# A graph network's edge pass: TensorE fetches the eighth tile of neighbour rows in two steps of three, by one-pass float32r products

## The reference, cut to what matters

```python
q = x @ Wq + bq ; k = x @ Wk + bk ; v = x @ Wv + bv ; e = eattr @ We
kj = k[src] + e                                   # rows of k fetched by source node
alpha = sum(q[dst] * kj, -1) / sqrt(C)
a = softmax of alpha over the edges of one destination
out = segment_sum(a * (v[src] + e), dst) + x @ Ws + bs
```

## Time and profile before

| | |
|---|---|
| runs, median of 3 | 6549.0 us (6548.15 to 6552.57) |
| the profiled execution's own time | 6551.77 us |
| its span | 6550.1 us |
| TensorE, matmul | 5681.8 us busy (87%) |
| VectorE | 4841.0 us (74%) |
| GpSimd | 4534.8 us (69%) |
| ScalarE | 2723.7 us (42%) |
| mean granted TensorE clock | 0.860 |

### The profile page before, as it was taken

How to read it: one execution, slowest core, us unless ns; L and a number is a source line. 1 busy time by engine, 2 the same in 40 slices (tenths; PEclk the granted TensorE clock), 3 DMA queues, 4 the chain that set the end, 5 groups by cost and what they waited for, 6 DMA issues and landing times. The chain is left out here.

```text
span 6550.1 us, 181005 instructions
## 1 busy us (share of the span) xinstructions
PE 5681.8 (87%) x44238; PEld 3448.3 (53%) x44238; DVE 4841.0 (74%) x17139; ACT 2723.7 (42%) x12085; POOL 4534.8 (69%) x4907
## 2 busy tenths in 40 slices
PE   7997888888888888888888888888888888888887
PEld 5775555555555555555555555555555555555554
DVE  6556777777777777777777777777777777777777
ACT  3223444444444444444444444444333333333332
POOL 1223777777777775777777777775777777777775
PEclk9998888888888888888888888888888888888887
DMA  4554333333333343333333333333333333333333
GB/s 128 159 159 107 98 98 98 98 98 98 98 98 100 96 100 101 98 98 99 98 98 99 99 97 99 97 99 101 100 98 98 98 98 98 98 98 98 98 98 81
DMA packets 710753, 668.87 MB, mean 102 GB/s; under 512 B 395660, under 2 KB 532814, under 8 KB 710702
## 3 DMA queue, kind: packets, MB, share of 16 engines
q0 software_dynamic: 154880, 306.75, 19.1%
q1 hardware_dynamic: 526730, 308.56, 17.7%
q10 hardware_dynamic: 29092, 52.97, 2.7%
HBM read 645.88 MB, written 21.78 MB: 102 GB/s over the span
## 5 line engine op out<-in xcount | busy, mean ns | idle before, releaser
L1830 POOL DMA_INDIRECT Gall<-KV,sdn x4638 | 4397.5, 948 | 1438.6 <-issue 1374.4
L1100 PE MATMUL pG<-KVS,oh 128*128 128x512 f32 (+1 forms) x5226 | 2971.0, 725 | 24.1 <-DVE lm L838 2.0
L1100 PEld LDWEIGHTS pG<-KVS,oh 128*128 128x128 f32 x5226 | 1200.6, 241 | 1404.9 <-issue 1390.7
L1141 ACT ACTIVATE vals<-vj,vals 128x32 f32<-128x32 f32 (+1 forms) x7960 | 1794.8, 312 | 19.3
L1134 ACT ACTIVATE vals<-dd 128x16 f32<-128x16 f32 (+1 forms) x606 | 131.7, 217 | 3247.0 <-DVE dd L963 3219.4
L884 DVE TENSOR_TENSOR kj<-Gall,pE 128x512 f32<-128x512 f32 x603 | 408.5, 678 | 477.3 <-DMA Gall<-KV,sdn 467.0
L1088 PE MATMUL pY<-O,vals 128*66 128x42 f32 (+1 forms) x10576 | 755.6, 233 | 0.0
L1088 PEld LDWEIGHTS pY<-O,vals 128*66 128x66 f32 (+1 forms) x10576 | 683.2, 139 | 47.0 <-ACT vals L1148 35.4
L1073 PE MATMUL pY<-fw,Ob 128*42 128x6 bf16 (+1 forms) x4800 | 211.1, 166 | 448.2 <-DVE cr L936 447.3
L873 DVE SCALAR_TENSOR_TENSOR oh<-kb,prow,pM 128x512 f32<-128x512 int16 (+1 forms) x606 | 472.4, 780 | 21.2 <-DMA kb<-K 19.0
L1021 PE MATMUL pE<-bd,ea 64*128 64x128 f32 x4848 | 465.8, 314 | 16.9 <-PEq L1414 16.2
(11 more groups left out here) (253 smaller groups left out, 6398.1 us busy)
## 6 DMA issues: line engine op xcount, KB each, us to landing
db<-D SPq DMA_DIRECT2D x606, 256.0 KB, 3.8
ea<-in_ea SPq DMA_DIRECT2D x606, 128.0 KB
Gall<-KV,sdn POOLq DMA_INDIRECT x4638
db<-D ACTq DMA_DIRECT2D x202, 256.0 KB, 3.6
qw<-QT SPq DMA_DIRECT2D x1818, 5.2 KB
dr<-in_dr SPq DMA_DIRECT2D x1212, 4.0 KB
ea<-in_ea SPq DMA_DIRECT2D x202, 64.0 KB, 3.5
sdn<-in_sdn SPq DMA_DIRECT2D x606, 12.0 KB
```

The source lines that it names most:

```text
L1100: p = e.matmul(pG[:, 0:128 * m], oh[s.slot][:, n, :], KVS[:, 4 * q:4 * q + m, :].rearrange("p t c -> p (t c)"), start=k == 0 and n == 0, s ...
L1141: i = e.activation(vals[u][:, j, C * h:C * h + C], vj[u][:, j, C * h:C * h + C], ACT.Identity, scale=vals[u][:, j, 64 + h:65 + h])
L1830: e.indirect_dma_start(G[u][:, j, :], None, kvtab, bass.IndirectOffsetOnAxis(ap=sdn[u][:, j:j + 1], axis=0)).then_inc(s_g[u], 16)
```

## The change

GpSimd leaves out the eighth gather in two blocks of three: blocks A (3, 6, ...) and B (4, 7, ...). Block A's pick ("early") is made a step ahead of the block, in stage Z between d and cont, and block B's where the pick was. There are two tables of keys (`kb[0]`, `kb[1]`) and two one-hot tables of 13 quads (`ohA`, `ohB`). In a step with block A in stage A, `p_gp` fetches quads 4 to 12 of B's fetch; with block B it waits for B's pick and fetches quads 0 to 8 of the next A fetch; with the third block a new operation `p_gq` behind q fetches A's quads 9 to 12, then, behind aT and A's pick, `p_gp` fetches quads 0 to 3 of B's. `v_oh` makes 9 quads in two of the steps and 4 + 4 in the third.

Each quad is now two products in float32r, one with the upper and one with the lower part of the table: `KVH` (in place of `KVS`) and `KVL` (over `hT`), made in the late loop by ScalarE (`upper_A`, `upper_in_place_A`) and VectorE (`lower_V`). As `hT` is overwritten, GpSimd sets its rows of ones again in the next table phase ("one"). VectorE's edge pass also waits for the end of ScalarE's table phase.

```diff
+    ohA = nc.alloc_sbuf_tensor_at("ohA", [128, QUADS, 128], F32R, offset=nc.sbuf_base - 256 * NT)
+    KVH = nc.alloc_sbuf_tensor_at("KVH", [128, NT, 128], F32R, offset=nc.sbuf_base - 512 * NT)
+    KVL = nc.alloc_sbuf_tensor_at("KVL", [128, NT, 128], F32R, offset=nc.sbuf_base - 512 * NT)
...
-    oh = [sb(f"oh{u}", [128, PIECE[2], 128]) for u in range(3)]
+    kb = [sb(f"kb{x}", [128, 128], I16) for x in "AB"]
+    ohB = sb("ohB", [128, QUADS, 128], F32R)
...
+        def upper_A(e, c):
+            if c >= 3:
+                e.wait_ge(own["A"], pA["kh", c - 3])
+            e.activation(part(c), KVS[:, cells(c), :], ACT.Copy).then_inc(own["A"], 1)
+
+        def upper_in_place_A(e, c):
+            e.wait_ge(own["V"], pV["kl", c])
...
+            e.activation(KVH[:, cells(c), :], part(c).bitcast(F32), ACT.Copy).then_inc(own["A"], 1)
...
+        def lower_V(e, c):
+            e.wait_ge(own["A"], pA["th", c])
+            e.wait_ge(own["P"], pP["qs", c])
+            e.tensor_tensor(KVL[:, cells(c), :], KVS[:, cells(c), :], part(c).bitcast(F32),
+                            ALU.subtract).then_inc(own["V"], 1)
...
-        first_pick = 2 + z.peel
-        pick_slot = first_pick % 3
+        pick_A, pick_B = 2 + z.peel, 3 + z.peel
+        slot_A, slot_B = pick_A % 3, pick_B % 3
...
         def picks(s):
 
-            return s.slot == pick_slot and not (isinstance(s.i, int) and s.c < first_pick)
+            return s.slot in (slot_A, slot_B) and not (isinstance(s.i, int) and s.c < first_of(s))
...
-            after(e, "P", "gp", s - 1)
+            if u == slot_A:
+                after(e, "P", "gq", s)
+            else:
+                after(e, "P", "gp", s - 1)
...
+        def hot(e, table, x, f, t):
+            return e.scalar_tensor_tensor(
+                table[:, f:t, :], kb[x][:, :].unsqueeze(1).to_broadcast([128, t - f, 128]), prow[:, 0:1],
+                pQd[:, f:t].unsqueeze(2).to_broadcast([128, t - f, 128]), ALU.subtract, ALU.is_equal)
+
         def v_oh(e, s):
...
+            if s.slot == slot_B:
+                key_landed(e, s + 2)
+                return hot(e, ohA, 0, 0, CUT_A)
+            if s.slot == slot_A:
+                return hot(e, ohB, 1, CUT_B, QUADS)
+            hot(e, ohA, 0, CUT_A, QUADS)
+            key_landed(e, s + 2)
+            return hot(e, ohB, 1, 0, CUT_B)
...
+        def fetch(e, table, f, t):
+            for n in range(f, t):
+                q = order_q[n]
+                m = min(4, NT - 4 * q)
+                for h, half in enumerate((KVH, KVL)):
+                    p = e.matmul(pG[:, 0:128 * m], table[:, n, :],
+                                 half[:, 4 * q:4 * q + m, :].rearrange("p t c -> p (t c)"),
+                                 start=n == 0 and h == 0, stop=n == QUADS - 1 and h == 1)
+            return p
+
         def p_gp(e, s):
...
+            if s.slot == slot_A:
+                return fetch(e, ohB, CUT_B, QUADS)
+            if s.slot == slot_B:
+                if picks(s):
+                    after(e, "V", "sel", s)
+                    hold(e)
+                return fetch(e, ohA, 0, CUT_A)
+            after(e, "V", "early", s + 1)
+            hold(e)
+            return fetch(e, ohB, 0, CUT_B)
+
+        def p_gq(e, s):
+            after(e, "V", "oh", s - 1)
+            hold(e)
+            return fetch(e, ohA, CUT_A, QUADS)
```

More of the change, by code:

```diff
@@ L7 @@
 F32 = mybir.dt.float32
+F32R = mybir.dt.float32r
 I32 = mybir.dt.int32
@@ L472, in node_phase @@
             if folds:
-                oG += [("clr", c) for c in fo]
+                oG += [(o, c) for c in fo for o in (("one", "clr") if kind == "mid" else ("clr",))]
                 for c in fo:
@@ L497, in node_phase @@
             oP += [(o, c) for o in q_P]
-            oA += [(o, c) for o in q_A]
-            oV += [(o, c) for o in q_V]
+            oA += [(o, c) for o in q_A + ["th"]] + ([("kh", c - 2)] if c >= 2 else [])
+            oV += [(o, c) for o in q_V + ["kl"]]
+        if late:
+            oA += [("kh", NG - 2), ("kh", NG - 1)]
         pV, pP, pA, pG_ = place(oV), place(oP), place(oA), place(oG)
@@ L556, in rows_P @@
             e.wait_ge(own["A"], pA["col", c])
+            if kind == "mid":
+                e.wait_ge(own["G"], pG_["one", c])
             if c >= 2:
@@ L593, in scalar @@
                 query_A(e, c)
+                upper_A(e, c)
+                if c >= 2:
+                    upper_in_place_A(e, c - 2)
+            if late:
+                upper_in_place_A(e, NG - 2)
+                upper_in_place_A(e, NG - 1)
         def columns_A(e, c):
@@ L612, in rows_A, with part @@
                          ACT.Copy).then_inc(own["A"], 1)
+        def part(c):
+            return ohB[:, 4 * (c % 3):4 * (c % 3) + tiles_of[c], :]
+        def upper_A(e, c):
[4 more added lines that the diff above has]
+            e.wait_ge(own["V"], pV["kl", c])
+            if c == 0:
+                for k in range(SL):
+                    e.wait_ge(s_kv[k], kv_landed[k])
+            e.activation(KVH[:, cells(c), :], part(c).bitcast(F32), ACT.Copy).then_inc(own["A"], 1)
         def query_A(e, c):
@@ L642, in pool @@
                 e.wait_ge(own["P"], pP["ftr", c])
+                if kind == "mid":
+                    if c:
+                        e.wait_ge(own["G"], pG_["clr", c - 1])
+                    e.memset(hT[64:128, 512 * c:512 * c + 128 * tiles_of[c]], 1.0).then_inc(own["G"], 1)
+                    e.wait_ge(own["G"], pG_["one", c])
                 e.memset(acc[:, 512 * c:512 * c + 128 * tiles_of[c]], 0.0).then_inc(own["G"], 1)
@@ L765, in edge_pass @@
         NL = 6 if att else 1
-        first_pick = 2 + z.peel
-        pick_slot = first_pick % 3
-        s_k = sem(f"{name}_k") if att else None
+        pick_A, pick_B = 2 + z.peel, 3 + z.peel
+        slot_A, slot_B = pick_A % 3, pick_B % 3
+        s_k = [sem(f"{name}_k{x}") for x in "AB"] if att else None
         sel_V = sem(f"{name}_sel") if att else None
@@ L847, in sel_at @@
         def sel_at(s, k):
-            return s.times(5, k + 1 - 5 * (first_pick // 3))
+            turn = 0 if s.slot == slot_A else 5
+            return s.times(10, turn + k + 1 - 10 * (first_of(s) // 3))
         def v_sel(e, s, inc, n):
@@ L880, in v_kj @@
             if picks(s):
-                after(e, "V", "sel", s)
+                after(e, "V", "early" if s.slot == slot_A else "sel", s)
             if opening(s):
@@ L1307, in tensor_drain @@
             p_q(e, s0, TT - 1).then_inc(dP, 1)
-            if TAIL == T:
-                e.wait_ge(dV, nV["sel0"])
-                hold(e)
+            after(e, "V", "oh", s0)
+            hold(e)
+            e.matmul(pG[:, 0:2], ohB[:, CUT_B, :], KVH[:, 0, 0:2], start=False, stop=True)
             after(e, "A", "vals", s3)
@@ L1416, in made, with picked_early @@
         def made(s):
-            return not isinstance(s.i, int) or s.c >= first_pick - 3
+            return not isinstance(s.i, int) or s.c >= pick_A - 2
+        def picked_early(s):
+            return picks(s) and s.slot == slot_A
         def vector_step(e, t, on):
@@ L1435, in vector_step @@
             if "A" in on:
-                if picks(at):
+                late = picks(at) and at.slot == slot_B
+                if late:
                     v_sel(e, at, pV, 1)
-                v_kj(e, at).then_inc(pV, 1 if picks(at) else 2)
+                v_kj(e, at).then_inc(pV, 1 if late else 2)
                 v_vj(e, at).then_inc(pV, 1)
@@ L1464, in vector_step @@
                 missing(e, "V", t, "d1", "d")
+            if picked_early(zt):
+                v_sel(e, zt, pV, 1)
             if "Z" in on:
-                v_cont(e, zt).then_inc(pV, 1)
+                v_cont(e, zt).then_inc(pV, 1 if picked_early(zt) else 2)
                 v_last(e, zt).then_inc(pV, 1)
             else:
-                missing(e, "V", t, "cont", "last")
+                missing(e, "V", t, "early", "last")
             if "A" in on:
@@ L1776, in sync_step @@
                 load_dr(e, s, b)
-            if att and picks(s + 2):
+            if att and picks(s + 2) and not (isinstance(s.i, int) and s.c + 2 == first_of(s + 2)):
                 load_keys(e, s + 2)
```

80 lines of the change are left out of this document (31 added, 49 removed).

## The result

| | before | after |
|---|---|---|
| runs, median of 4 | 6549.44 us (6548.15 to 6552.57) | 7001.43 us (6985.68 to 7008.21) |
| the profiled execution's own time | 6551.77 us | 6985.68 us |
| its span | 6550.1 us | 6984.0 us |
| ratio | | 1.0686, 95% interval [1.0666, 1.0706] |
| TensorE, matmul | 5681.8 us | 6011.7 us (86%) |

The change makes the kernel 6.9% slower. The direction was forecast, the size was not: 6730 us with an upper end of 6990.

The account below looks back on a forecast made before the run. VectorE and its TensorE waits would bound: 27.46 + 2.0 = 29.5 us a triple (three consecutive blocks), 0.75 above 28.75, +149 us over 198 triples. With 34 at layer starts, 6551.8 becomes 6735, stated as 6730; range 6300 to 6990.

Parts of the forecast that it names:

- rival A: The forecast itself: VectorE paces, with waits of 1.1 to 3.3 us, 28.6 to 30.8 us a triple, 6560 to 6990; chance 0.48.
- The signs: Expected profile: 4440 gathers, gathered-row wait under 100 us, VectorE busy 5600, pick and fhi waits 400 or more, clock 0.8 to 0.9.
- Tables and picks: VectorE's own work: one-hot tables 3.98 instead of 2.11 us a triple, a second pick 1.90 more, 27.46 in all.
- the narrow pairs show no larger fixed part: TensorE's fetch: pairs of 128-column products, eight in 1.06 us, taken as support for 0.213 us per one-pass product.
- rival D: A fetch product is dearer than its columns: at 0.427 us each, 7160 and up, 7600 to 8000 with waits; chance 0.17.
- rival D's second case: Weight load not hidden, 0.40 us a fetch product: 30.4 us a triple plus waits for picks, 6900 to 7600 us.
- Waits for TensorE: VectorE's waits at late pick, fhi and early pick: 2.0 us a triple taken, bounds 0 and 6.5.
- (a): VectorE at the late pick, behind a fetch of 17 full-width products: waits nothing, or 2.7 us at low clock.
- (b): VectorE at fhi in the step after the late pick, behind 18 fetch products: waits nothing or 2.8 us.
- (c): VectorE at the early pick, behind the eight products of gq: waits nothing or 1 us.
- Layer starts: Longer table phases: VectorE and TensorE wait for ScalarE's end, 11.4 us later, three times, 34 us.
- B: GpSimd stays the bound, faster, if the clock stays high and waits are below 1 us: 6307 to 6530; chance 0.27.

Follow-up runs that it names:

- before_busy2_b: The kernel before the change, with two unused float32 products of 208 columns added on TensorE in every step: 6564.51 us against 6562.15, ratio 1.0005.
- the disturbed runs: Runs of several kernels in which every kernel of which there are both kinds took 2,860 to 3,880 us more; the kernel before took 9676 to 9746 us.

## Why the prediction was right and wrong

*The bound, right.* GpSimd was the bound, the cover went, VectorE with its waits took its place (rival A, to which 0.48 was given). The signs came: 4440 gathers, 35.9 us of waiting ahead of kj (under 100 forecast), VectorE busy 5529.8 (5600), picks and fw 652 us (400 or more), 10,398 records, clock 0.84.

*Tables and picks, right.* The table of nine quads takes 1.40 us (3518.41; about 1.45 forecast), the new type costs VectorE nothing, and VectorE's 27.46 us a triple are seen nearly bare in the kernel with filled holes: 27.6 in two triples with the clock at 1.00 throughout.

*A fetch product, 0.213 forecast and 0.229 measured.* The step "the narrow pairs show no larger fixed part" failed: they are float32, and the 15 ns belong to the one-pass four-byte type, as the products at the layers' ends show. By 17 products it is 0.3 us at the late fetch. The sign set for rival D, a pitch above 0.23, was missed by 1 ns. The load of weights, 0.23 to 0.25 us in the mean and 0.19 at 2.4 GHz, is hidden in this pitch, as the trace of before let one expect. The Trainium skill ("TensorE: Matmul & The Clock Gate", The mechanism) lets a load overlap a running product only on another row group; the same section also names a background weight buffer as a target for which a load is pulled ahead. By the first it should not be hidden here, since load and product use the same rows of the array; with the 0.40 us that this would give, rival D's second case, the trace of after does not agree: it has 0.229.

*Waits for TensorE, 2.0 us a triple forecast and 3.3 measured: this is the step that failed.* The share of time at the low clock was right, a third (0.84). What failed is "with the clock low in a third of the cases as now", which spread it evenly over (a), (b) and (c). The two low stretches of a triple recur at the same places, (a)'s and (b)'s fetches, while gq's eight products and the eight behind the early pick run at 2.4 GHz, so that (c) never came. (a) came 192 times in 198 at 2.0 us each, instead of one time in three at 2.7; (b) 199 times at 1.4 us, instead of one in three at 2.8. The prediction had what it takes to see this: it names the holes in which TensorE waits for VectorE as what brings the low clock, and such holes have fixed places in a triple; but then it prices the waits as chances. The timeline of TensorE in the kernel before shows the same pair of holes, a long fetch at the low clock right behind them, and the first hole again in the next triple:

```profile
3002.33 0.34 PE L1073 MATMUL pY<-fw,Ob 128*42 128x6 bf16 x8 [1.32 <-DVE cr L936]
...
3004.08 0.37 PE L1053 MATMUL pS<-ident,al 128*16 128x128 f32 x1 [0.74 <-DVE d L958]
3004.57 6.46 PE L1100 MATMUL pG<-KVS,oh 128*128 128x512 f32 x8
...
3029.17 0.34 PE L1073 MATMUL pY<-fw,Ob 128*42 128x6 bf16 x8 [1.32 <-DVE cr L936]
```

And the earlier trace rows have VectorE wait at 167 of the 198 picks, far more than one in three, though not all of these waits need the low clock: with the clock at 0.92 (before_busy2_b) it waits at all 198, 1.2 us each. In the profiled execution 1.3 us a triple are 257 us, and the layer starts take back 15: nearly all of the 251 between 6735 and 6985.68.

*Layer starts, 34 us forecast and 18.6 measured.* The phases got longer as forecast, by about half; which of the extra copies are hidden was not tried.

*The rivals.* B, GpSimd or VectorE at 27.5 us without waits, is what the change can give, once its condition is made to hold: 6307 to 6530 was its range, 6392 the kernel with filled holes. The condition ("waits below 1 us") was named rightly, and could have been brought about. The range ended at 6990, 30.8 us a triple; the measured triple is 30.8 too, the profiled execution lies 4 us within that end and the median 11 us beyond it.

What stays open: why three products in every step leave low clock at more late fetches than two, and why every fresh placement settles where it does. That the holes were needed at both places was not tried apart.

## What to carry to other kernels

When an engine that hid the others' waits is relieved, the waits left over must be laid out at their places in the cycle, not multiplied by a mean share of low clock: this loop settled into one pattern, in which the low clock fell on the same work nearly every time. If TensorE stands still twice in a row just ahead of a long stream that another engine waits for, try to fill these holes with products that nobody reads, and only these: six in the holes gave 6392 us, six spread evenly 6592, nine spread evenly 6734. And a low mean clock is no fault to mend as long as no other engine waits for what runs in it: 0.75 was the fastest kernel here, which leaves out half of the fetch's products.

## What the hardware showed that was not expected

A one-pass float32r product of 512 columns starts every 0.229 us in the fetch at 2.4 GHz, and every 0.427 at 1.2 GHz; the 0.213 of its columns is missed by 15 ns, which the width of the weights does not change and bfloat16 does not have. At 1.2 GHz, where 512 columns are 0.427, nothing of it is left.

Adding work to an engine shortened a kernel by 409 and by 609 us, through its clock.

In the disturbed runs TensorE stood still ahead of single instructions for nothing that the profile shows, while the fetch ran through unbroken (timeline of TensorE, nine products in the holes):

```profile
5007.10 0.24 PE L1131 MATMUL pY<-fw,Ob 128*42 128x6 bf16 x4 [0.92 <-issue]
5007.72 0.21 PE L1131 MATMUL pY<-fw,Ob 128*42 128x6 bf16 x2 [0.38 <-issue]
5009.16 0.23 PE L1131 MATMUL pY<-fw,Ob 128*42 128x6 bf16 x2 [1.23 <-issue]
```

In the undisturbed run with six products in the holes all eight of these products start in one block (3512.32 above). What causes the stalls can't be told from these traces.
